# Mixture-of-experts feed-forward on one core: row blocks gathered six ahead into four buffers, three output buffers, and a first run of TensorE products on a tile of ones

## The chip, the cores and the metric

The kernel runs on one core of a Trainium2 chip. A core has a matrix engine (TensorE, PE in the profile, with PEld for its weight loads), VectorE (DVE), ScalarE (ACT), GpSimd (POOL) and SyncE (SP), which here only issues transfers. The metric is the device time of one execution in microseconds; for each kernel the median of its runs is given. The kernel before took 495.78 us (median of 3 runs, 494.04 to 497.90).

## What is computed

The input has 64 batch entries of 64 tokens with 256 features: 4096 tokens. A linear layer with eight low-rank corrections, weighed per batch entry by the condition, gives h. A router picks two of eight experts for each token; an expert is a gated MLP of width 352. A shared MLP of width 704 runs on every token. The output is the input plus both.

```
h      = x @ W_base.T + b_base + 2 * sum_e cond[b, e] * (x @ A_e.T) @ B_e.T
scores = softmax(h @ gate_w.T);  top two, weights normalised, times 2.5
routed = sum over the two experts e: w_e * (silu(h @ w_gate[e]) * (h @ w_up[e])) @ w_down[e]
shared = (silu(h @ sw_gate) * (h @ sw_up)) @ sw_down
out    = x + routed + shared
```

All of it is in float32. Most products are made of three cheaper ones: each operand is split into a high part in a rounded 32-bit format (`_h`) and a low part (`_l`), and `three_pass` (L285) adds high x high, low x high and high x low.

## The kernel before, in words

The program is written out by hand for each engine, and semaphores tie the engines together. An engine runs its instructions in the order written; a wait holds back everything behind it on that engine.

**Start.** SP and ACT issue the loads of the weights (`a_raw`, `base_raw`, `b_raw`) and of the first tokens (`xin`). GpSimd fills the identity tile `ident` (L481, L482). When it is ready, TensorE makes `WARM` = 12 transposes of `ident` into a PSUM bank that nobody reads (L625 to L627). Then it transposes `a_raw` (L632), the first 512 tokens (L640), the gate's weights, the condition and `base_raw` (L654), and makes small float32 products that fold the gate into the linear layer (L658). Those need `gate_t`, which ACT copies after the high parts of the first tokens (`x_high(0)`, L895).

**Projection.** Eight groups of 512 tokens (L677). DVE adds the bias, ACT splits each float32 into two 16-bit halves, and SP writes them to the DRAM tensor `x1_dram`, a row per token.

**Shared MLP, first part.** 5 of the 8 groups go through the shared MLP (L778), each in six chunks. Its sums go by way of `y_sb`, four tiles of 128 x 256 (L145), to `base_dram`; `s_base` counts those stores. Meanwhile DVE works out the routing: `tok_i`, which tokens stand in each block of 128 rows, and `dst_i`, where each row of results goes.

**Routed blocks.** 71 blocks (`NBLK`) of 128 rows, each of one expert. For block i:

- POOL `gather(i)` (L562) fetches the rows by an indirect transfer into `rows[i % 3]`; from block 3 on it waits first for the transpose that read this buffer last (`s_turn`).
- SP `turn_rows(i)` (L349) waits for the gather (`s_row`) and until the words of block i - 2 have been read (`s_rlo`, `s_rhi`), and transposes the rows by DMA into `turned[i % 2]`.
- DVE `r_word_low` (L1354) and ACT `r_word_high` (L1009) put the halves together in `rt_w`; ACT `r_high` and DVE `r_low` split it again for the products.
- PE `e_gate_up(i)` (L806): 12 products, first the gate's, then the up ones. ACT `e_silu` (L1028) and DVE `e_mul` (L1394) follow, the latter into `g`. PE `e_turn_g(i)` (L799) transposes `g`, ACT `e_high` and DVE `e_low` split it, and PE `e_down(i)` (L821) makes the down products. The order on PE is: `e_turn_g(i-1)`, `e_gate_up(i)`, `e_down(i-1)`.
- DVE `e_y(i)` (L1401) adds the two halves of the result into `y_sb[i % 4]`, and POOL `scatter(i)` (L569) writes it to `y_dram` by an indirect transfer. `e_y` of a block from 4 on waits until the scatter of four blocks earlier has landed (`s_sc`); before that it waits for `s_base`.

POOL first issues five gathers; then for each i `gather(i + 5)`, eight times a piece of other work (i = 14 to 21), and `scatter(i)` (L577 to L584).

**End.** The last three groups go through the shared MLP (L870) while SP loads back the routed rows (`load_sums`, L422), once all scatters have landed (L444). DVE adds them in, and the results are stored.

Of the kernel before, what the change touches and what calls it, by code (L numbers as in the profile page):

```python
# [21 lines left out]
def adaln_moe(nc, x, cond, w_base, b_base, lora_a, lora_b, gate_w, w_gate, w_up, w_down,  # L22
              sw_gate, sw_up, sw_down, out):
    NB, SEQ, D = x.shape
    E, RANK, _ = lora_a.shape
# [10 lines left out]
    NBLK = (TOPK * T + E * (P - 1)) // P  # L36
# [3 lines left out]
    TG = GT // P  # L40
# [10 lines left out]
    NPG = 5  # L51
# [2 lines left out]
    UP = NPRE + NBLK  # L54

    TURN = 12
    WARM = 12

    RANK_AT, HOT_AT = 4, 9

# [14 lines left out]
    x1_dram = nc.dram_tensor("x1_halves", (T, 2 * D), U16, kind="Internal").ap()  # L75
# [4 lines left out]
    with ExitStack() as ctx:  # L80
        def sb(name, shape, dt=F32, where=ctx):
            return where.enter_context(nc.sbuf_tensor(name, shape, dt))

        def sem(name):
            return ctx.enter_context(nc.semaphore(name))

        bank = [ctx.enter_context(nc.psum_tensor(f"bank{i}", [P, 512], F32)) for i in range(8)]


        ident = sb("ident", [P, P])  # L90
# [34 lines left out]
        act = sb("act", [P, GT])  # L125
# [13 lines left out]
        rows = [sb(f"rows{i}", [P, 2 * D], U16) for i in range(3)]  # L139
        turned = [sb("turned0", [P, 2 * K, P], U16), turned1]  # L140
# [3 lines left out]
        rt_l = [sb(f"rt_l{i}", [P, D], F32R) for i in range(2)]  # L144
        y_sb = sb("y_sb", [P, TG, D])  # L145

        GU, DN = K * 2 * F, FC * D
# [64 lines left out]
        s_cond, s_gate, s_ath, s_atl, s_wer = (sem(f"s_{n}") for n in ("cond", "gate", "ath", "atl", "wer"))  # L214
        s_wah, s_wal, s_bh, s_bl, s_bg = (sem(f"s_{n}") for n in ("wah", "wal", "bh", "bl", "bg"))
        s_xin = [sem(f"s_xin{i}") for i in range(2)]
        s_xfirst = sem("s_xfirst")
        s_tx, s_txh, s_txl = sem("s_tx"), sem("s_txh"), sem("s_txl")
        s_H, s_hw, s_hwh, s_hwl = sem("s_H"), sem("s_hw"), sem("s_hwh"), sem("s_hwl")
        s_p, s_x1, s_half = sem("s_p"), sem("s_x1"), sem("s_half")  # L220
# [10 lines left out]
        s_res, s_base = sem("s_res"), sem("s_base")  # L231
        s_r, s_exp, s_exp_in = sem("s_r"), sem("s_exp"), sem("s_exp_in")
        s_mark, s_sums, s_rank = sem("s_mark"), sem("s_sums"), sem("s_rank")
        s_ids, s_hot, s_perm, s_routed, s_blk = sem("s_ids"), sem("s_hot"), sem("s_perm"), sem("s_routed"), sem("s_blk")
        s_row = [sem(f"s_row{i}") for i in range(3)]
        s_turn = [sem(f"s_turn{i}") for i in range(2)]
        s_rlo, s_rhi, s_rth, s_rtl, s_gT_e = sem("s_rlo"), sem("s_rhi"), sem("s_rth"), sem("s_rtl"), sem("s_gT_e")
        s_y = sem("s_y")
        s_sc = [sem(f"s_sc{i}") for i in range(4)]
        s_acc = [sem(f"s_acc{j}") for j in range(NG)]  # L240
        s_mix, s_emix, s_out = sem("s_mix"), sem("s_emix"), sem("s_out")

# [11 lines left out]
        EG, EU, TB, YE = bank[0], bank[1], bank[2], bank[6:8]  # L254
# [53 lines left out]
        def _(sp):  # L308
# [39 lines left out]

            def turn_rows(i):  # L349

                sp.wait_ge(s_row[i % 3], 16 * (i // 3 + 1))
                if i >= 2:
                    sp.wait_ge(s_rlo, i - 1)
                    sp.wait_ge(s_rhi, i - 1)
                sp.dma_start_transpose(turned[i % 2][:], rows[i % 3][:]).then_inc(s_turn[i % 2], 16)


            for h, got in enumerate((s_xfirst, s_xin[0])):
# [55 lines left out]
            for i in range(4):  # L414
                turn_rows(i)
            store_base(NPG - 1)
            for i in range(4, NBLK):
                turn_rows(i)
# [22 lines left out]
            sp.wait_ge(s_D, UP)  # L441
            sp.wait_ge(s_base, 16 * NPG)
            load_raw(NPG + 1, raw_p)
            for i in range(4):  # L444
                sp.wait_ge(s_sc[i], 16 * ((NBLK - i + 3) // 4))
            load_sums(NPG)
            load_sums(0)
            load_sums(NPG + 1)
# [15 lines left out]
            for n, (first, end) in ((0, (0, 2)), (2, (3, 4))):  # L464
                sp.wait_ge(s_fin, 2 * last + n + 1)
                r = last * GT
# [5 lines left out]
        def _(pool):  # L472
# [68 lines left out]
            src, d, step = mark, 1, 0  # L541
            while d < NT:
# [3 lines left out]
                src, d, step = dst, 2 * d, step + 1  # L546
# [13 lines left out]


            def gather(i):  # L562
                if i >= 3:
                    pool.wait_ge(s_turn[(i - 3) % 2], 16 * ((i - 3) // 2 + 1))
                pool.indirect_dma_start(rows[i % 3][:], None, x1_dram,  # L565
                                        bass.IndirectOffsetOnAxis(ap=tok_i[:, i:i + 1], axis=0)
                                        ).then_inc(s_row[i % 3], 16)

            def scatter(i):  # L569
                pool.wait_ge(s_y, i + 1)  # L570
                pool.indirect_dma_start(y_dram, bass.IndirectOffsetOnAxis(ap=dst_i[:, i:i + 1], axis=0),  # L571
                                        y_sb[:, i % 4, :], None).then_inc(s_sc[i % 4], 16)

            pool.wait_ge(s_routed, 1)
            for i in range(2):
                pool.wait_ge(s_x1st[i], 16 * (NG // 2))
            for i in range(5):  # L577
                gather(i)
            for i in range(NBLK):
                if i + 5 < NBLK:  # L580
                    gather(i + 5)
                if 14 <= i < 14 + 4 * K:
                    split_low_part(NPG, *divmod(i - 14, 4))
                scatter(i)  # L584
# [4 lines left out]
        def _(pe):  # L589
# [32 lines left out]
                           b_h[:], b_l[:], False, True, skip=True).then_inc(s_p, 1)  # L622


            pe.wait_ge(s_ident, 1)  # L625
            for _ in range(WARM):
                pe.transpose(bank[5][:, 0:P], ident[:], ident[:])  # L627


            pe.wait_ge(s_da, 16)  # L630
# [25 lines left out]
            for k in range(K):  # L656
                for o in range(K):
                    mm = pe.matmul(bank[2 + k][:, D:DX], base_raw[:, o, k * P:(k + 1) * P], gate_t[:, o * E:(o + 1) * E],  # L658
                                   start=(o == 0), stop=(o == K - 1))
# [203 lines left out]
            i = n_turns * TURN + 2  # L863
# [219 lines left out]

        @block.vector
        def _(v):
            v.wait_ge(s_dcond, 16)
            v.tensor_scalar(cond_er[:].rearrange("b (e r) -> b e r", e=E),
                            cond_in[:].rearrange("b (e r) -> b e r", r=1).broadcast_to([NB, E, RANK]),
# [311 lines left out]

            def e_y(i):  # L1401
                v.wait_ge(s_D, UE + i + 1)
                if i < 4:
                    v.wait_ge(s_base, 16 * NPG)
                else:
                    v.wait_ge(s_sc[i % 4], 16 * (i // 4))
                v.tensor_reduce(y_sb[:, i % 4, :], YE[i % 2][:, 0:2 * D].rearrange("p (h d) -> p d h", h=2), AX.X, ALU.add).then_inc(s_y, 1)  # L1407

            r_word_low(1)
            e_mul(0)  # L1410
# [78 lines left out]
```

## Time and profile before

| | before |
|---|---|
| runs | 494.04, 495.78, 497.90 us |
| the profiled execution | 496.81 us, span on the core 495.0 us |
| PE busy | 486.6 us, 98% |
| DVE, ACT, POOL busy | 71%, 53%, 45% |
| DMA | 74.53 MB, mean 151 GB/s |

A row of the timeline gives the start in the span, the duration, engine, line, operation and tiles, with "xN" for merged instructions, and in brackets how long the engine sat idle before and what ended that. Several products can be in flight: the distance between two starts is what one costs in a row, its duration is longer. The start-up takes the first 8 us of the span, the routed blocks lie between about 178 and 424 us.

### The profile page before, as it was taken

What the parts mean: (1) busy time and instruction counts of PE and PEld (TensorE: products, weight loads), DVE (VectorE), ACT (ScalarE), POOL (GpSimd) and SP (SyncE); (2) the same over time, 40 slices, a digit from 0 to 9 for tenths busy, and PEclk for the clock granted to TensorE, in tenths of its full rate; (3) what the DMA queues carried; (4) which work ended last, traced back from release to release, by engine and by line L of the source; (5) the groups of instructions that cost most, each with busy time, mean ns of one, the idle gap of its engine ahead of it and who ended that gap; (6) DMA issues with size and microseconds to landing.
All of it is one profiled execution on the core that took longest, in us unless ns stands there. A gap on an engine that the chain in (4) does not pass through costs nothing.

```text
span 495.0 us, 9758 instructions
## 1 busy us (share of the span) xinstructions
PE 486.6 (98%) x3069; PEld 448.7 (91%) x3070; DVE 349.8 (71%) x785; ACT 261.8 (53%) x526; POOL 220.3 (45%) x231
## 2 busy tenths in 40 slices
PE   8999999999999999899999998999999999999997
PEld 7999988888888899899999998999999999888886
DVE  3557866888886556676777766667766776479896
ACT  3577876666562445475555544555555553444322
POOL 2042338564640444565776555565556552211100
PEclk9999999999999999999999999999999999999999
DMA  7497579372222244444444443444444442599942
GB/s 201 153 299 224 172 204 329 118 219 86 44 85 44 86 106 121 116 118 117 127 118 117 117 126 96 122 115 115 127 117 119 117 118 65 154 376 310 384 159 85
DMA packets 104952, 74.53 MB, mean 151 GB/s; under 512 B 61962, under 2 KB 99860, under 8 KB 104916
## 3 DMA queue, kind: packets, MB, share of 16 engines
q1 hardware_dynamic: 97712, 55.20, 38.4%
q0 software_dynamic: 6816, 18.62, 12.6%
q8 instruction: 17, 0.28, 0.2%
q10 hardware_dynamic: 388, 0.27, 0.2%
q14 instruction: 19, 0.16, 0.1%
HBM read 40.25 MB, written 20.32 MB: 122 GB/s over the span
## 4 chain that ended last, share of the span: by engine, by line
PE 93%; DMA 2%; DVE 2%; issue 1%; ACT 1%; SPq 0%; POOL 0%; DVEq 0%; another core or an unknown queue 0%; POOLq 0%
PE bank L286 22%; PE bank L288 22%; PE bank L287 22%; PE bank L831 10%; PE bank L833 5%; PE bank L803 5%; DMA pick<-y_rows 1%; PE bank L596 1%; PE bank L608 1%; PE bank L604 1%; DMA y_rows<-y_sb,dst_i 1%; PE bank L605 1%; PE bank L741 1%; PE bank L740 1%; DVE acc L1432 1%
## 5 line engine op out<-in xcount | busy, mean ns | idle before, releaser
L571 POOL DMA_INDIRECT y_rows<-y_sb,dst_i x71 | 70.0, 985 | 84.1 <-DVE y_sb L1407 83.8
L286 PE MATMUL bank<-w_all,rt_h 128*128 x284 | 97.5, 343 | 0.0
L288 PE MATMUL bank<-w_all,rt_l 128*128 x284 | 91.6, 323 | 0.0
L287 PE MATMUL bank<-w_all,rt_h 128*128 x284 | 91.5, 322 | 0.0
L565 POOL DMA_INDIRECT rows<-x_halves,tok_i x71 | 68.7, 968 | 25.0 <-issue 21.1
L831 PE MATMUL bank<-w_all,gt_h 128*128 (+1 forms) x213 | 78.1, 397 | 0.0
L1001 ACT CAST gt_h<-bank 128x512 fp32r<-128x512 f32 (+1 forms) x47 | 27.5, 585 | 85.7 <-DVE bank L1310 77.1
L286 PE MATMUL bank<-xs_h,sg_h 128*128 128x512 f32 x176 | 70.4, 400 | 0.0
L287 PE MATMUL bank<-xs_l,sg_h 128*128 128x512 f32 x176 | 68.9, 391 | 0.0
L288 PE MATMUL bank<-xs_h,sg_l 128*128 128x512 f32 x176 | 68.7, 390 | 0.0
L1394 DVE TENSOR_TENSOR g<-bank,act 128x352 f32<-128x352 f32 x71 | 37.2, 525 | 42.3 <-issue 33.8
L1023 ACT CAST gt_h<-bank 128x384 fp32r<-128x384 f32 x71 | 34.0, 479 | 58.1 <-issue 38.4
L1407 DVE TENSOR_REDUCE y_sb<-bank 128x256 f32<-128x512 f32 x71 | 49.0, 690 | 17.4 <-issue 9.7
L833 PE MATMUL bank<-w_all,gt_l 128*128 (+1 forms) x213 | 59.6, 280 | 0.0
L511 POOL TENSOR_TENSOR w_all<-w_own,w_all 128x704 fp32r<-128x704 f32 (+2 forms) x32 | 42.7, 1359 | 32.7 <-ACT w_all L913 32.7
L1014 ACT COPY rt_w<-turned 128x256 uint16<-128x256 uint16 x71 | 34.6, 487 | 41.5 <-PE bank L288 21.3
L287 PEld LDWEIGHTS bank<-w_all,rt_h 128*128 128x128 f32 x284 | 53.6, 189 | 0.0
L286 PEld LDWEIGHTS bank<-w_all,rt_h 128*128 128x128 f32 x284 | 53.5, 189 | 0.1
L288 PEld LDWEIGHTS bank<-w_all,rt_l 128*128 128x128 f32 x284 | 53.4, 188 | 0.0
L1398 DVE TENSOR_TENSOR gt_l<-bank,gt_h 128x384 fp32r<-128x384 f32 x71 | 39.5, 557 | 11.7 <-ACT gt_h L1023 5.7
L517 POOL TENSOR_TENSOR xs_l<-xs_w,xs_h 128x512 fp32r<-128x512 f32 x14 | 18.3, 1308 | 65.6 <-ACT xs_h L935 65.6
L831 PEld LDWEIGHTS bank<-w_all,gt_h 128*128 128x128 f32 (+1 forms) x213 | 40.0, 188 | 6.8 <-issue 0.5
(192 smaller groups left out, 1114.4 us busy)
## 6 DMA issues: line engine op xcount, KB each, us to landing
pick<-y_rows SPq DMA_DIRECT2D x16, 512.0 KB, 7.8
x_halves<-x_half SPq DMA_DIRECT2D x8, 512.0 KB, 3.3
xin<-in_x_dram SPq DMA_DIRECT2D x7, 512.0 KB, 4.8
w_own<-in_L_ffn_w_gate_dram SPq DMA_DIRECT2D x8, 352.0 KB, 4.2
w_own<-in_L_ffn_w_up_dram SPq DMA_DIRECT2D x8, 352.0 KB, 4.7
y_sb<-in_x_dram SPq DMA_DIRECT2D x5, 512.0 KB, 3.4
base_rows<-y_sb SPq DMA_DIRECT2D x5, 512.0 KB, 2.8
acc<-base_rows SPq DMA_DIRECT2D x5, 512.0 KB, 7.5
```

The source lines that it names most:

```text
L286: pe.matmul(o, lh, rh, start=start, stop=False, skip_group_check=skip)
L287: pe.matmul(o, lh, rl, start=False, stop=False, skip_group_check=skip)
L288: return pe.matmul(o, ll, rh, start=False, stop=stop, skip_group_check=skip)
L511: pool.tensor_tensor(lo, own_ap, hi.bitcast(F32), ALU.subtract).then_inc(s_wlo, 1)
L565: pool.indirect_dma_start(rows[i % 3][:], None, x1_dram, bass.IndirectOffsetOnAxis(ap=tok_i[:, i:i + 1], axis=0)).then_inc(s_row[i % 3], 16)
L571: pool.indirect_dma_start(y_dram, bass.IndirectOffsetOnAxis(ap=dst_i[:, i:i + 1], axis=0), y_sb[:, i % 4, :], None).then_inc(s_sc[i % 4], 16)
L831: pe.matmul(YE[par][:, 0:2 * D].rearrange("p (h d) -> p h d", h=2), gt_h[par][0:n, cols], both, start=(c == 0), stop=False, skip_group_che ...
L833: mm = pe.matmul(YE[par][:, 0:D], gt_l[par][0:n, cols], high, start=False, stop=(c == FC - 1), skip_group_check=True)
L1014: sc.copy(words[:, :, :, 1], turned[i % 2][:, K:2 * K, :]).then_inc(s_rhi, 1)
L1394: v.tensor_tensor(g[:, 0:F], EU[:, 0:F], act[:, 0:F], ALU.mult).then_inc(s_g, 1)
L1398: v.tensor_tensor(gt_l[i % 2][:, 0:FC * P], TB[:, 0:FC * P], gt_h[i % 2][:, 0:FC * P].bitcast(F32), ALU.subtract).then_inc(s_gl, 1)
L1407: v.tensor_reduce(y_sb[:, i % 4, :], YE[i % 2][:, 0:2 * D].rearrange("p (h d) -> p d h", h=2), AX.X, ALU.add).then_inc(s_y, 1)
```

## The change

There are two edits.

**The routed blocks' buffers.** The fourth tile of `y_sb` becomes a fourth buffer for gathered rows, so three are left for outputs (`N_Y` = 3). Six gathers are issued first, then `gather(i + 6)` ahead of `scatter(i)`. Block i uses row buffer i for i < 3, and (i + 1) % 4 after that, so block 6 is the first in the shared tile; its gather waits for `s_base` in place of a transpose. From block 7 on `gather(i)` waits for the transpose of block i - 4. `e_y(i)` waits for the scatter of block i - 3.

**The first products.** TensorE no longer waits for `ident` first. DVE fills 128 columns of `act` with 1.0 as its first instruction, and TensorE makes 14 plain products act x act into the same unread bank; only then it waits for `ident`.

```diff
-    WARM = 12
+    WARM = 14
+        N_Y = TG - 1
+        row_bufs = [r[:] for r in rows] + [y_sb[:, N_Y, :].bitcast(U16)]
+
+        def rows_of_block(i):
+            return row_bufs[i if i < 3 else (i + 1) % 4]
...
-                sp.wait_ge(s_row[i % 3], 16 * (i // 3 + 1))
+                sp.wait_ge(s_row[i % 4], 16 * (i // 4 + 1))
...
-                sp.dma_start_transpose(turned[i % 2][:], rows[i % 3][:]).then_inc(s_turn[i % 2], 16)
+                sp.dma_start_transpose(turned[i % 2][:], rows_of_block(i)).then_inc(s_turn[i % 2], 16)
...
             def gather(i):
-                if i >= 3:
-                    pool.wait_ge(s_turn[(i - 3) % 2], 16 * ((i - 3) // 2 + 1))
-                pool.indirect_dma_start(rows[i % 3][:], None, x1_dram,
+                if i == 6:
+                    pool.wait_ge(s_base, 16 * NPG)
+                elif i >= 3:
+
+                    had = i - 3 if i < 6 else i - 4
+                    pool.wait_ge(s_turn[had % 2], 16 * (had // 2 + 1))
+                pool.indirect_dma_start(rows_of_block(i), None, x1_dram,
...
-            for i in range(5):
+            for i in range(6):
                 gather(i)
             for i in range(NBLK):
-                if i + 5 < NBLK:
-                    gather(i + 5)
+                if i + 6 < NBLK:
+                    gather(i + 6)
...
+            pe.wait_ge(s_warm, 1)
+            for _ in range(WARM):
+                pe.matmul(bank[5][:, 0:P], act[:, 0:P], act[:, 0:P], start=True, stop=True)
             pe.wait_ge(s_ident, 1)
-            for _ in range(WARM):
-                pe.transpose(bank[5][:, 0:P], ident[:], ident[:])
...
         def _(v):
+            v.memset(act[:, 0:P], 1.0).then_inc(s_warm, 1)
             v.wait_ge(s_dcond, 16)
...
-                if i < 4:
+                if i < N_Y:
                     v.wait_ge(s_base, 16 * NPG)
                 else:
-                    v.wait_ge(s_sc[i % 4], 16 * (i // 4))
+                    v.wait_ge(s_sc[i % N_Y], 16 * (i // N_Y))
```

PE at the start of the program, of the kernel before (a row is a line, the operation, output and inputs, sizes, and "xN" for repeats):

```order
L588 UNCONDITIONAL_BRANCH
L627 MATMUL bank<-ident 128x128 x12
L632 MATMUL bank<-ident,a_raw 128x128 x2
L640 MATMUL bank<-ident,xin 128x128 x8
L645 MATMUL bank<-ident,g_raw 128x8 x2
```

The same place in the changed kernel, whose lines are numbered about ten higher:

```order
L598 UNCONDITIONAL_BRANCH
L637 MATMUL bank<-act 128x128 x14
L643 MATMUL bank<-ident,a_raw 128x128 x2
L651 MATMUL bank<-ident,xin 128x128 x8
L656 MATMUL bank<-ident,g_raw 128x8 x2
```

Twelve transposes have become fourteen products; nothing else on PE has another order.

POOL from its first gather on, in the kernel before; a DMA into `rows` is a gather and one into `y_rows` a scatter, and the semaphore each waits for stands in brackets:

```order
L565 DMA rows<-x_halves,tok_i 128x512 [waits s_x1st1,s_x1st0,s_routed]
L565 DMA rows<-x_halves,tok_i 128x512 x2
L565 DMA rows<-x_halves,tok_i 128x512 [waits s_turn0]
L565 DMA rows<-x_halves,tok_i 128x512 [waits s_turn1]
L565 DMA rows<-x_halves,tok_i 128x512 [waits s_turn0]
L571 DMA y_rows<-y_sb,dst_i 17408x256 [waits s_y]
L565 DMA rows<-x_halves,tok_i 128x512 [waits s_turn1]
L571 DMA y_rows<-y_sb,dst_i 17408x256 [waits s_y]
L565 DMA rows<-x_halves,tok_i 128x512 [waits s_turn0]
L571 DMA y_rows<-y_sb,dst_i 17408x256 [waits s_y]
```

The same place in the changed kernel, where a gather into the shared tile reads `y_sb<-`:

```order
L575 DMA rows<-x_halves,tok_i 128x512 [waits s_x1st1,s_x1st0,s_routed]
L575 DMA rows<-x_halves,tok_i 128x512 x2
L575 DMA rows<-x_halves,tok_i 128x512 [waits s_turn0]
L575 DMA rows<-x_halves,tok_i 128x512 [waits s_turn1]
L575 DMA rows<-x_halves,tok_i 128x512 [waits s_turn0]
L575 DMA y_sb<-x_halves,tok_i 128x512 [waits s_base]
L581 DMA y_rows<-y_sb,dst_i 17408x256 [waits s_y]
L575 DMA rows<-x_halves,tok_i 128x512 [waits s_turn1]
L581 DMA y_rows<-y_sb,dst_i 17408x256 [waits s_y]
L575 DMA rows<-x_halves,tok_i 128x512 [waits s_turn0]
```

The gather of block 6 has moved ahead of the scatter of block 0, and so every later gather stands one scatter earlier. The transposes that they wait for stand at the same places between the scatters as before.

## Rows read from the trace of the kernel before

**Rows 1.** The page: busy time by engine; chain that ended last, by engine.

```profile
PE 486.6 (98%) x3069; PEld 448.7 (91%) x3070; DVE 349.8 (71%) x785; ACT 261.8 (53%) x526; POOL 220.3 (45%) x231
...
PE 93%; DMA 2%; DVE 2%; issue 1%; ACT 1%; SPq 0%; POOL 0%; DVEq 0%; another core or an unknown queue 0%; POOLq 0%
```

**Rows 2.** Waits of PE: engine, line, releaser: us in total, times, longest.

```profile
PE bank L803 <- DVE g L1394: 3.2, 2, 1.6
PE bank L627 <- POOL ident L482: 1.5, 1, 1.5
```

**Rows 3.** Timeline of the first 8.6 us: start, duration, engine, line, operation, tiles.

```profile
0.80 0.09 POOL L480 MEMSET spare<- 1x4 f32 x1 [0.29 <-POOLq L1479]
...
0.84 0.21 POOL L481 MEMSET ident<- 128x128 f32 x1
1.12 0.29 POOL L482 TENSOR_SCALAR_AFFINE_SELECT ident<-ident 128x128 f32<-128x128 f32 x1
...
1.47 2.82 PE L627 MATMUL bank<-ident 128*128 128x128 f32 x12 [1.47 <-POOL ident L482]
...
4.21 0.29 PEld L632 LDWEIGHTS bank<-ident,a_raw 128*128 128x128 f32 x2 [0.33 <-DMA a_raw<-in_L_cond_As_dram]
...
5.21 0.22 DVE L1087 TENSOR_SCALAR cond_er<-cond_in 64x128 f32<-64x128 f32 x1 [5.21 <-DMA cond_in<-in_cond_dram]
...
6.27 1.07 ACT L895 CAST xt_h<-bank 128x512 fp32r<-128x512 f32 x2 [0.96 <-PE bank L640]
...
7.48 0.97 PEld L658 LDWEIGHTS bank<-gate_t,base_raw 128*128 128x128 f32 x8 [0.30 <-ACT gate_t L944]
```

**Rows 4.** By line: xcount, duration in ns min/median/max, first and last start in us.

```profile
L627 PE MATMUL bank<-ident x12: 421/421/476, 1.5 to 3.9; 128*128 128x128 f32 x12
...
L640 PE MATMUL bank<-ident,xin x8: 273/421/421, 4.7 to 6.1; 128*128 128x128 f32 x8
...
L658 PEld LDWEIGHTS bank<-gate_t,base_raw x8: 186/192/192, 7.5 to 8.3; 128*128 128x128 f32 x8
L658 PE MATMUL bank<-gate_t,base_raw x8: 256/256/277, 7.5 to 8.3; 128*128 128x8 f32 x8
...
L596 PE MATMUL bank<-ident,xin x56: 272/272/307, 12.4 to 54.2; 128*128 128x128 f32 x56
```

**Rows 5.** The page, granted clock in 40 slices; timeline of eight transposes in the projection.

```profile
PEclk9999999999999999999999999999999999999999
...
12.25 0.94 PEld L596 LDWEIGHTS bank<-ident,xin 128*128 128x128 f32 x8
```

**Rows 6.** Critical chain, two of the projection's eight groups of tokens (start, duration, engine, line).

```profile
23.08 0.23 PE bank L604
...
29.80 0.23 PE bank L604
...
36.51 0.23 PE bank L604
```

**Rows 7.** Timeline of PE: the first long wait, and two blocks after it.

```profile
202.98 0.55 PE L803 MATMUL bank<-ident,g 128*128 128x128 f32 x3 [1.60 <-DVE g L1394]
...
206.34 0.49 PE L803 MATMUL bank<-ident,g 128*128 128x128 f32 x3
206.59 0.41 PE L286 MATMUL bank<-w_all,rt_h 128*128 x1
...
209.65 0.49 PE L803 MATMUL bank<-ident,g 128*128 128x128 f32 x3
```

**Rows 8.** Timeline of DVE, ACT and POOL around that wait and behind it.

```profile
199.52 0.41 DVE L1363 TENSOR_TENSOR rt_l<-rt_w,rt_h 128x256 fp32r<-128x256 f32 x1
202.40 0.53 DVE L1394 TENSOR_TENSOR g<-bank,act 128x352 f32<-128x352 f32 x1 [2.46 <-issue]
...
204.56 0.42 DVE L1363 TENSOR_TENSOR rt_l<-rt_w,rt_h 128x256 fp32r<-128x256 f32 x1
...
206.54 0.69 DVE L1407 TENSOR_REDUCE y_sb<-bank 128x256 f32<-128x512 f32 x1
...
200.76 0.46 ACT L1028 ACTIVATE act<-bank 128x352 f32<-128x352 f32 x1 [1.44 <-PE bank L288]
...
207.51 0.99 POOL L571 DMA_INDIRECT y_rows<-y_sb,dst_i  x1 [1.25 <-DVE y_sb L1407]
```

**Rows 9.** Waits for gathered and turned rows: of SP in the span's 173 to 420 us, and of ACT in all.

```profile
SPq L355 <- DMA rows<-x_halves,tok_i: 25.6, 14, 3.0
...
ACT rt_w L1014 <- DMA turned<-rows: 14.0, 18, 1.6
```

**Rows 10.** Critical chain from the last scatter's issue until it has landed.

```profile
423.82 3.76 DMA y_rows<-y_sb,dst_i
```

More of the change, by code:

```diff
@@ L216, in adaln_moe @@
         s_xin = [sem(f"s_xin{i}") for i in range(2)]
-        s_xfirst = sem("s_xfirst")
+        s_xfirst, s_warm = sem("s_xfirst"), sem("s_warm")
         s_tx, s_txh, s_txl = sem("s_tx"), sem("s_txh"), sem("s_txl")
@@ L234, in adaln_moe @@
         s_ids, s_hot, s_perm, s_routed, s_blk = sem("s_ids"), sem("s_hot"), sem("s_perm"), sem("s_routed"), sem("s_blk")
-        s_row = [sem(f"s_row{i}") for i in range(3)]
+        s_row = [sem(f"s_row{i}") for i in range(4)]
         s_turn = [sem(f"s_turn{i}") for i in range(2)]
@@ L238, in adaln_moe @@
         s_y = sem("s_y")
-        s_sc = [sem(f"s_sc{i}") for i in range(4)]
+        s_sc = [sem(f"s_sc{i}") for i in range(N_Y)]
         s_acc = [sem(f"s_acc{j}") for j in range(NG)]
@@ L443, in _ @@
             load_raw(NPG + 1, raw_p)
-            for i in range(4):
-                sp.wait_ge(s_sc[i], 16 * ((NBLK - i + 3) // 4))
+            for i in range(N_Y):
+                sp.wait_ge(s_sc[i], 16 * ((NBLK - i + N_Y - 1) // N_Y))
             load_sums(NPG)
@@ L562, in gather @@
             def gather(i):
-                if i >= 3:
-                    pool.wait_ge(s_turn[(i - 3) % 2], 16 * ((i - 3) // 2 + 1))
-                pool.indirect_dma_start(rows[i % 3][:], None, x1_dram,
+                if i == 6:
[4 more added lines that the diff above has]
+                pool.indirect_dma_start(rows_of_block(i), None, x1_dram,
                                         bass.IndirectOffsetOnAxis(ap=tok_i[:, i:i + 1], axis=0)
-                                        ).then_inc(s_row[i % 3], 16)
+                                        ).then_inc(s_row[i % 4], 16)
             def scatter(i):
@@ L571, in scatter @@
                 pool.indirect_dma_start(y_dram, bass.IndirectOffsetOnAxis(ap=dst_i[:, i:i + 1], axis=0),
-                                        y_sb[:, i % 4, :], None).then_inc(s_sc[i % 4], 16)
+                                        y_sb[:, i % N_Y, :], None).then_inc(s_sc[i % N_Y], 16)
             pool.wait_ge(s_routed, 1)
@@ L1402, in e_y @@
                 v.wait_ge(s_D, UE + i + 1)
-                if i < 4:
+                if i < N_Y:
                     v.wait_ge(s_base, 16 * NPG)
                 else:
-                    v.wait_ge(s_sc[i % 4], 16 * (i // 4))
-                v.tensor_reduce(y_sb[:, i % 4, :], YE[i % 2][:, 0:2 * D].rearrange("p (h d) -> p d h", h=2), AX.X, ALU.add).then_inc(s_y, 1)
+                    v.wait_ge(s_sc[i % N_Y], 16 * (i // N_Y))
+                v.tensor_reduce(y_sb[:, i % N_Y, :], YE[i % 2][:, 0:2 * D].rearrange("p (h d) -> p d h", h=2), AX.X, ALU.add).then_inc(s_y, 1)
             r_word_low(1)
```

## The prediction, made before the changed kernel ran

> **What bounds the kernel.** I read the page's busy times first, then the chain that ended last, then the waits of TensorE, and only then the timelines of the two places that the change touches. TensorE is busy for 486.6 of 495.0 us, and it makes up 93% of the chain [rows 1]. So the reader should ask of each edit one thing: does it let TensorE start its work earlier, do less, or wait less? TensorE's own list of waits is short: 1.5 us for the identity tile at the start, and 3.2 us in two waits for `g` in the routed blocks [rows 2]. The rest of what it is not busy lies behind its last product. Between these, the blocks follow each other at TensorE's own pace: 206.34 to 209.65 us is 3.31 us for a block [rows 7], and 71 blocks of that are 235 us. An edit to the row buffers can win at most the 3.2 us. In the projection the same products come again every 6.72 us (23.08, 29.80, 36.51) [rows 6]: also TensorE's pace, with no slack into which a late start could disappear.
>
> **Row and output buffers.** The transposes that the gathers wait for are the same at each place of POOL's order: at the place ahead of `scatter(i)` both kernels wait for the transpose of block i + 2, and what is fetched there is block i + 5 before and block i + 6 after. So rows stand ready one block, 3.3 us, earlier. Who was late for them? SP waited 14 times, 25.6 us, for gathers, and ACT 18 times, 14.0 us, at most 1.6 us, for turned rows [rows 9]. That is real waiting, but it is covered: `rt_l` of the next block is done at 204.98 (204.56 + 0.42) and TensorE takes it at 206.59 [rows 7, 8], 1.6 us later, and no wait of TensorE in the list ends on `rt_l`. The edit removes covered waits, worth 0. Without that cover each us of lateness beyond it would be a us of TensorE's.
>
> Do the two waits of 1.6 us go? In the first, `rt_l` was finished at 199.93, before the stall; ACT then started the activation late at 200.76, and DVE the product for `g` at 202.40 with nothing that the profile names as its releaser [rows 8]. Neither instruction reads gathered rows or `y_sb`. I take 0; the far bound is -3.2 us.
>
> The price is one output buffer less. The reduce of a block starts at 206.54, its scatter is issued at 207.51 [rows 8], and a scatter takes 3.76 us from issue to landing [rows 10]: 211.27, 4.7 us after the reduce began. The third block after it wants the buffer at 206.54 + 3 x 3.31 = 216.5, so 5.2 us remain; with four buffers it was 8.5. Cost 0. The gather of block 6, now ahead of the first scatter, waits for `s_base`, for which the first `e_y` waits as well; it holds that scatter up by its issue, about 1 us, the same length as the 0.99 of a scatter's [rows 8], well inside the 5.2. The later gathers merely change places with the scatter ahead of them in POOL's queue.
>
> **The first products.** What is gained: DVE is idle until 5.21, so its fill can start when POOL's first own instruction does, at 0.80. POOL's fill of the same size took 0.21, a DVE operation on half the partitions 0.22 [rows 3]; I take 0.20. From the end of the identity (1.12 + 0.29 = 1.41) to the first transpose (1.47) went 0.06 [rows 3]. So the first product starts at 0.80 + 0.20 + 0.06 = 1.06, 0.41 us earlier.
>
> What is paid: the kind of product. The twelve transposes start from 1.5 to 3.9, 11 distances, 0.218 us each [rows 4]. A transpose shows as one record. But L658 is four float32 products in the code, and the trace has eight weight loads and eight products for it [rows 4]: a plain float32 product is two records. Eight of these in a row lie (8.3 - 7.5) / 7 = 0.115 us apart [rows 4], no closer than the eight transposes of L596, of which (0.94 - 0.14) / 7 = 0.115 us [rows 5]. They have only 8 moving columns, so the weight load seems to set the distance; with 128 columns a record can't cost less than that, and as the transposes with 128 columns cost no more, I give each record a transpose's distance. 14 products are then 28 records, where there were 12.
>
> Next the clock. The page prints full granted clock for all slices [rows 5], which hides the start; the durations show it: 421 ns for a transpose at first and 272 later, 0.218 us apart and then 0.115, so TensorE ran at 1.2 GHz and then at 2.4. From the weight load at 4.21 [rows 3] to the last of the ten transposes of L632 and L640 at 6.1 there are nine distances, 1.89 us; n x 0.218 + (9 - n) x 0.115 = 1.89 gives n = 8.3, so the clock rose at about 6.0, 4.5 us after the first transpose, and nothing but transposes had run. After the change I take it at the same distance from the first product, 5.56, or at the same instant, 6.0.
>
> The sum, rise at 5.56: (5.56 - 1.06) / 0.218 = 20.6 records at the slow pace, 7.4 x 0.115 = 0.85 for the others, so L632's successor starts at 6.41 instead of 4.21. Its ten transposes then all run fast; the last starts 9 x 0.115 = 1.03 later, at 7.45, against 6.1: **+1.35 us**. Rise at 6.0: 22.7 records, 5.3 x 0.115 = 0.61, 6.61, 7.65: +1.55. I take +1.4. The load of `a_raw` no longer matters; it was there at 4.21 [rows 3]. What hangs on the transposes, ACT's copy at 6.27 and through `gate_t` L658 at 7.48 [rows 3], moves along, and no later stage gives it back, as TensorE's pace rules there.
>
> Bounds for this term: if the clock were up from the first product, 28 x 0.115 = 3.2, L632 at 4.28, the last transpose at 5.3: -0.8 us. No row shows such a start. The upper bound is the rival below, +4.5.
>
> One rule of the Trainium skill speaks to the price. "TensorE: Matmul & The Clock Gate", in its table of terms, says that transpose mode is "4× faster for FP32". The trace shows two records a product where it shows one for a transpose, at equal distances, which is a factor of 2 for the 8 columns it has; no row has a plain float32 product of 128 columns, so the factor of 4 is open. By the rule the sum would be that of the fourfold rival.
>
> **The sum.** 0 for the buffers + 1.4 for the first products. The profiled execution took 496.81 us, so 498.2 for one like it. It lies 1.03 above the median of 495.78; against the median: 495.78 + 1.4 = **497.2 us**.
>
> **Rivals.**
> (1) *A product costs one transpose.* 14 x 0.218 = 3.05, the row ends at 4.11, L632 starts with `a_raw` at 4.21 as before, and the clock rises 0.4 earlier: 6.2 distances slow, 2.8 fast, the last transpose at 5.88: -0.2 us, 495.6. Against it stand the eight records for four products.
> (2) *A product costs four transposes*, 0.87 slow and 0.46 fast. 4.5 / 0.87 = 5.2 products before the rise, 8.8 x 0.46 = 4.05 after it: 9.6, the last transpose at 10.65: +4.5 us, 500.3. For it: 128 columns instead of 8 may cost each record twice. Against it: in transposes the 128 columns hide behind the weight load.
> (3) *The earlier rows cure the two stalls*, that is, they came from late rows: -3.2 + 1.4 = -1.8, 494.0. Against it: `rt_l` was ready, see above. If the rows edit did that and the start cost nothing, it would be 492.6, still within 1%.
> (4) *Clearly slower: the three output buffers.* If `y_sb` waits for the scatter of three blocks before, TensorE waits too, since `e_down` waits for `s_y` two blocks back. It decides from 9.9 us (3 x 3.31) between reduce and landing; it takes 4.7 now. At 10.2 us a block would cost 3.4 instead of 3.31, 68 blocks x 0.09 = +6 us, 503. Only twice the landing time would do it, and the load on the transfers does not rise.
> (5) *The change does nothing*: both effects under what runs scatter, 495.8.
>
> **Chances and range.** Forecast (+1.4, spread 496.3 to 498.6 with the 1.55 case and the scatter of a median) 0.55; (1) and (5) 0.16; (2) 0.12; (3) 0.10; (4) 0.03; the rest, something unseen of either sign, 0.04. A measurement here can't tell less than about 1%, 5 us, from no change. Below 490.8 lies only unseen gain: 0.03. Above 500.7 lie (4), part of (2) and the unseen: 0.07. Within: 0.90. The range leaves out (4) and the outer parts of (2) and (3): 494.4 to 500.0.
>
> **What would show it.** In the changed kernel's trace: the products on `act` as 28 records, 0.218 us apart and then 0.115, the first at about 1.06; L632's successor at about 6.4 instead of 4.21; `gate_t` products at about 8.8 instead of 7.48, and every later mark 1.4 later. 14 records would make (1) right, distances of 0.4 or more (2). In the blocks: SP's and ACT's waits for rows shrink towards nothing, the block stays at 3.31 us, and POOL's and DVE's waits for `s_sc` don't appear. I am wrong if TensorE's waits for `g` vanish together with the late rows, if the clock is already up in the first products, or if a wait of TensorE for `y_sb` turns up.

## The result, and the profile after

The changed kernel takes 501.01 us (median of 6 runs, 499.76 to 501.81), the kernel before beside it 495.28 (6 runs, 493.35 to 498.57): 5.7 us more, ratio 1.010 with a 95% interval of 1.0064 to 1.0137. The forecast was 497.2 and no measurable change, its range ended at 500.0. The slower time lies outside. The ratios, here and in the table below, are taken from the runs no more than 1.5% above the fastest of the same kernel; in the second series this leaves out 15 of the 35 runs of the kernel before (the other 20 have a median of 498.08) and 3 of the 12 of start_again (the other 9: 501.81), elsewhere at most one run of a kernel.

A difference in microseconds is one of medians. The recorded ratio is not the quotient of the two medians, and can differ from it: after_third's medians are 1.8 us apart, its ratio of 1.0049 would be 2.4.

The profiled execution took 501.19 us with a span of 499.2, against 496.81 and 495.0. The busy times of the page, to be held against [rows 1], and TensorE's waits, against [rows 2]:

```profile
PE 489.0 (98%) x3085; PEld 451.0 (90%) x3086; DVE 349.9 (70%) x786; ACT 262.5 (53%) x526; POOL 221.2 (44%) x231
```

```profile
PE bank L814 <- DVE g L1406: 3.2, 2, 1.7
PE bank L814 <- issue: 1.5, 2, 0.9
PE bank L637 <- DVE act L1097: 1.1, 1, 1.1
PE bank L292 <- DVE gt_l L1331: 0.6, 1, 0.6
```

There are 16 more instructions on PE (28 records for 12), and two more kinds of wait stand in the list: 1.5 us ahead of the transposes of `g` (L814, which was L803) without a releaser that the profile names, and 0.6 us near the end. The start, to be held against [rows 3]:

```profile
0.90 0.17 DVE L1097 MEMSET act<- 128x128 f32 x1 [0.90 <-PEq L1491]
1.12 5.58 PEld L637 LDWEIGHTS bank<-act 128*128 128x128 f32 x28 [0.79 <-DVE act L1097]
...
6.62 0.25 PEld L643 LDWEIGHTS bank<-ident,a_raw 128*128 128x128 f32 x2
...
9.12 0.97 PEld L669 LDWEIGHTS bank<-gate_t,base_raw 128*128 128x128 f32 x8 [0.31 <-ACT gate_t L955]
```

The products need the time up to 6.6; `a_raw`, there at 4.21 before, waits for TensorE now. The weight loads of L669 start at 9.12 against 7.48: 1.64 us late. The loss of 4.2 us of span falls in three places: 1.6 at the start; some 2.0 in the routed blocks (the first transposes of `g` come 1.6 us later than before, the last ones 3.6); and 0.6 after them. The three places in the blocks where TensorE stood longest:

```profile
205.41 0.55 PE L814 MATMUL bank<-ident,g 128*128 128x128 f32 x3 [1.66 <-DVE g L1406]
...
375.25 0.55 PE L814 MATMUL bank<-ident,g 128*128 128x128 f32 x3 [0.94 <-issue]
...
383.67 0.55 PE L814 MATMUL bank<-ident,g 128*128 128x128 f32 x3 [1.59 <-DVE g L1406]
```

The first is the counterpart of the wait at 202.98 [rows 7]: in both kernels it stands ahead of the transposes of block 5 (the blocks counted from 0). The other wait of the kernel before, at 304.11, is gone, and two others have come: the second row stands behind block 55, the third two blocks further on. Rows are not late there. SP's waits in the routed blocks (span 173 to 420) show that they are early:

```profile
SPq L360 <- DVE rt_w L1371: 110.5, 52, 4.1
SPq L360 <- ACT rt_w L1025: 5.1, 3, 2.8
```

The 25.6 us for gathers of [rows 9] are gone, and SP waits for the words of block i - 2 instead: the gathered rows lie ready and the two `turned` buffers are what is scarce. ACT's 14.0 us for turned rows, 18 waits, are down to 2.0 us in two waits.

### The profile page after: what moved, and what is told of

Same layout as the page of the kernel before. It is cut to its first block, busy times and chain, and to the rows that moved or that the text cites. A ratio compares the mean times of both kernels' runs of the same rounds, so it can differ in the third digit from the quotient of the medians.

```text
span 499.2 us, 9791 instructions
## 1 busy us (share of the span) xinstructions
PE 489.0 (98%) x3085; PEld 451.0 (90%) x3086; DVE 349.9 (70%) x786; ACT 262.5 (53%) x526; POOL 221.2 (44%) x231
## 4 chain that ended last, share of the span: by engine, by line
PE 92%; DMA 2%; DVE 2%; issue 2%; ACT 0%; SPq 0%; another core or an unknown queue 0%; DVEq 0%
PE bank L292 22%; PE bank L293 22%; PE bank L294 22%; PE bank L842 10%; PE bank L844 5%; PE bank L814 5%; DMA pick<-y_rows 1%; PE bank L606 1%; PE bank L637 1%; DMA y_rows<-y_sb,dst_i 1%; PE bank L618 1%; PE bank L614 1%; PE bank L615 1%; PE bank L752 1%; PE bank L751 1%
## 5 line engine op out<-in xcount | busy, mean ns | idle before, releaser
L575 POOL DMA_INDIRECT rows<-x_halves,tok_i x54 | 52.5, 973 | 19.5 <-DMA turned<-rows 10.2
```

Of the source, the lines that this page charges most:

```text
L575: pool.indirect_dma_start(rows_of_block(i), None, x1_dram, bass.IndirectOffsetOnAxis(ap=tok_i[:, i:i + 1], axis=0)).then_inc(s_row[i % 4], 16)
```

## Experiments

A series is a set of kernels run in turn with the kernel before, on one chip. The series differ: in some the kernel before lies within 492 to 494 us nearly always (quiet), in others it scatters by 5 to 15 us. I speak of quiet chips and chips that stall, but that it is the chip, and not the hour, is not shown: only one chip was used twice (third and last series), and was quiet both times. In the profiles the difference lies in stalls of 1 to 2 us in the routed blocks. It turned out to decide what the change costs, so each row names its series. The start_warm28 and no_warm rows rest on four runs each. "First", "second", "third" and "fourth" in the expectations are the series that hold the changed kernel itself.

| series, kernel before (median, lowest to highest, runs) | kernel | median us | ratio to before (95%) |
|---|---|---|---|
| first, 495.28 (493.35 to 498.57, 6) | changed kernel | 501.01 | 1.0100 (1.0064 to 1.0137) |
| parts, quiet, 492.79 (491.77 to 496.83, 29) | start_only | 494.26 | 1.0042 (1.0025 to 1.0059) |
| | start_warm7 | 492.83 | 1.0011 (0.9995 to 1.0026) |
| | rows_only | 493.02 | 1.0003 (0.9979 to 1.0027) |
| | outputs3_only | 492.73 | 1.0001 (0.9992 to 1.0011) |
| second, 500.86 (494.0 to 508.92, 35) | after_again | 503.04 | 1.0047 (1.0017 to 1.0078) |
| | both_warm7 | 501.59 | 1.0058 (1.0014 to 1.0101) |
| | start_again | 503.13 | 1.0057 (1.0007 to 1.0106) |
| | rows_again | 501.63 | 1.0041 (1.0007 to 1.0074) |
| third, quiet, 492.84 (491.8 to 496.21, 12) | after_third | 494.65 | 1.0049 (1.0035 to 1.0063) |
| | ident_products | 494.55 | 1.0025 (1.0003 to 1.0048) |
| | start_warm28 | 499.49 | 1.0135 (1.0115 to 1.0156) |
| | no_warm | 496.53 | 1.0081 (1.0066 to 1.0097) |
| fourth, 495.64 (493.47 to 501.22, 23) | before_copy | 495.65 | 0.9997 (0.9964 to 1.0029) |
| | after_fourth | 500.55 | 1.0094 (1.0063 to 1.0126) |
| | both_warm7_again | 499.18 | 1.0063 (1.0039 to 1.0087) |
| last, quiet, 492.74 (491.71 to 496.47, 27) | rows_third | 492.73 | 1.0008 (0.9997 to 1.0019) |
| | outputs3_again | 492.83 | 1.0004 (0.9995 to 1.0013) |
| | rows_scatter_first | 492.69 | 0.9988 (0.9969 to 1.0007) |

### The parts alone

The start edit alone, in the kernel before:

```diff
-    WARM = 12
+    WARM = 14
+            pe.wait_ge(s_warm, 1)
+            for _ in range(WARM):
+                pe.matmul(bank[5][:, 0:P], act[:, 0:P], act[:, 0:P], start=True, stop=True)
             pe.wait_ge(s_ident, 1)
-            for _ in range(WARM):
-                pe.transpose(bank[5][:, 0:P], ident[:], ident[:])
...
+            v.memset(act[:, 0:P], 1.0).then_inc(s_warm, 1)
```

> The start edit alone: 14 products of ones, three row buffers and four output buffers as before. The changed kernel's trace shows 28 records of products and every later mark of the projection 1.6 us later, but the whole is 5.7 us slower in the median. Theory A (the start costs its 1.65 us and no more; the rest of the loss is made by the row buffers): +1.6 us, 497. Theory B (the start edit costs everything, because a later stage falls out of step): +5.7, 501. Theory C (two small costs and the scatter of the runs): +1.6 here and about +2 with the rows edit alone.

+1.5 us: theory A's number, and theory B is dead for a quiet chip. The same with 7 products:

```diff
-    WARM = 14
+    WARM = 7
```

> The start edit alone with 7 products in place of 14, so 14 records. If a record costs the distance of a transpose (0.2 us at first), the row of them ends at about 4.1 us and the load of a_raw, there at 4.2, comes last again: 0 to -0.3 us against before by theories A and C (the shift of the start is all that the edit does). Theory B has no reason for a loss either if it hangs on the shift; if it hangs on plain products or on the tile of ones as such, it stays 3 to 5 us slower.

No difference. So the loss hangs on the number of products. The products' own rows, of start_warm7 and then of start_only (x, duration min/median/max in ns, first and last start in us):

```profile
L627 PEld LDWEIGHTS bank<-act x14: 288/333/333, 1.1 to 3.8; 128*128 128x128 f32 x14
```

```profile
L627 PEld LDWEIGHTS bank<-act x28: 192/270/333, 1.1 to 5.6; 128*128 128x128 f32 x28
```

Fourteen records for 7 products, 28 for 14. The last of the 28 starts here at 5.6, in the changed kernel of the first series at 6.5: more of them fell into the fast clock (12 of the distances are 0.11 us here, 3 there).

The buffer edit alone is the changed kernel with the old start:

```diff
+            pe.wait_ge(s_ident, 1)
+            for _ in range(WARM):
+                pe.transpose(bank[5][:, 0:P], ident[:], ident[:])
-            pe.wait_ge(s_warm, 1)
-            for _ in range(WARM):
-                pe.matmul(bank[5][:, 0:P], act[:, 0:P], act[:, 0:P], start=True, stop=True)
-            pe.wait_ge(s_ident, 1)
...
-            v.memset(act[:, 0:P], 1.0).then_inc(s_warm, 1)
```

> The buffer edit alone: six gathers ahead into four buffers, three for outputs, with the twelve transposes of the identity at the start as before. Theory A: +4 us, 499, with TensorE's waits in the routed blocks grown by as much in most profiles (the changed kernel's profile has 6.3 us over 70 regular blocks, that of the kernel before 4.3). Theory B: 0. Theory C: about +2.

Nothing, on this chip. And the half of it that takes an output buffer away, with gathers as before:

```diff
-                if i < 4:
+                if i < N_Y:
...
-                    v.wait_ge(s_sc[i % 4], 16 * (i // 4))
-                v.tensor_reduce(y_sb[:, i % 4, :],
+                    v.wait_ge(s_sc[i % N_Y], 16 * (i // N_Y))
+                v.tensor_reduce(y_sb[:, i % N_Y, :],
```

> Three output buffers alone: gathers as before, five ahead into three buffers, and the fourth tile of y_sb left idle in the routed blocks. If the loss of the buffer edit comes from waits for a free output, it is here too, as large as in the buffer edit alone. If it comes from the gathers that run one block further ahead (other transfers at other times, GpSimd's scatters behind a gather's wait), this one takes 0 against before. My reading of the slack (5 us) says 0.

Nothing either. TensorE's list of waits in rows_only holds no wait in the blocks at all. Theory A's +4 us and theory C's +2 for the buffer edit both missed here. The parts add up to +1.5 to +2, not to 5.7.

### The whole again, on a chip that stalls

> The changed kernel itself, unaltered, again beside the kernel before. Alone, the start edit has cost 1.5 us in the median and a ratio of 1.0042, and the buffer edit nothing. Theory A (the two edits add up, and the rest of the 5.7 us measured first were stalls of 1.7 us that fell on its executions more often): +1.5 to +2, ratio 1.003 to 1.005, and its profile has no or few late semaphores of TensorE. Theory D (the two edits together make something that neither makes alone, a stage that falls out of step): +5 or more, ratio 1.010 or more, with waits of TensorE in the routed blocks in most executions.

> Both edits, with 7 products in place of 14 (14 records, which end at about 4.1 us, before a_raw is there). Theory A: the start costs nothing any more, so the kernel is as fast as before, ratio 0.998 to 1.002. Theory D, an interaction of the buffers with products of ones at the start: slower by 3 us or more still.

> The start edit alone once more, in the same series as the changed kernel, to compare the two directly. Theory A: the same time as the changed kernel within 0.5 us, ratio to before about 1.004. Theory D: 3 us or more below the changed kernel.

> The buffer edit alone once more, in the same series. Theory A: ratio 0.998 to 1.002. If the buffer edit makes the kernel more liable to stalls where the chip has them, the median or the highest time is above that of the kernel before by 2 us or more; the number of executions over 494.5 us tells it, where the kernel before had 3 of 29 in the last series.

The kernel before now took 501 us in the median and scattered from 494 to 509. The changed kernel was 2.2 us slower, as theory A has it, but both edits with 7 products came out at 1.0058 and the buffer edit alone at 1.0041, where A says 1.000. Against the 498.08 named with the result, the medians of the changed kernel, of both edits with 7 products and of the buffer edit alone are 5.0, 3.5 and 3.6 us up, which is what the fourth series will show; but start_again's 501.81 is 3.7 up too, where its edit explains 1.6. With intervals of plus or minus 0.4% this series can't decide, and I did not settle on A.

### What the row of products costs

> The changed kernel unaltered, a third series. The first gave ratio 1.0100 (1.0064 to 1.0137), the second 1.0047 (1.0017 to 1.0078). Theory A (1.6 us of start, the rest stalls that don't belong to the edits): ratio 1.003 to 1.005, +1.5 to +2.5 us. Theory D (a real loss of 4 us or more): 1.008 or more.

1.0049 on a quiet chip, +1.8 us: there the changed kernel costs what its start costs.

```diff
-                pe.transpose(bank[5][:, 0:P], ident[:], ident[:])
+                pe.matmul(bank[5][:, 0:P], ident[:], ident[:], start=True, stop=True)
```

> The kernel before with one word changed: the twelve first instructions are products of ident with ident in place of transposes. Nothing starts earlier, only the kind changes: 24 records in place of 12. If the kind is what costs: the records run to about 6.3 instead of 3.9 us with the clock up at 5.9 as in the profile of before, and the whole is 1.0 to 1.6 us slower. If the loss of the start edit came from the tile of ones or from VectorE's fill: no change.

+1.7 us in the median by this one word. Neither the tile of ones nor VectorE is to blame, the kind of product is. Its row, 24 records for 12 products and up to 5.7, where the 12 transposes of [rows 4] end at 3.9:

```profile
L627 PEld LDWEIGHTS bank<-ident x24: 192/333/338, 1.5 to 5.7; 128*128 128x128 f32 x24
```

Doubling the row (`WARM = 28` in start_only):

> The start edit alone with 28 products in place of 14, 56 records. By the theory that only the length of this row counts, 28 more records at the fast distance of 0.11 us add 3.1 us to the +1.5 of 14 products: +4.6 against before, ratio about 1.009. If a later wait took up a late start, it would be less.

+6.6 us, more than the 4.6 expected. The start is as worked out: `a_raw`'s transposes at 9.00, where the kernel before has them at 4.2. The rest stands in the profile as waits in the routed blocks, where start_only had none:

```profile
PE bank L832 <- DVE gt_l L1400: 2.7, 3, 1.4
```

VectorE makes `gt_l`, and the trace names what had held VectorE up. Ahead of the first of the three waits it was the first `e_y`, which waits for the last store out of `y_sb` (`s_base`), 2.60 us where start_only has 1.20. Ahead of the last it was a wait for turned rows:

```profile
194.21 0.69 DVE L1409 TENSOR_REDUCE y_sb<-bank 128x256 f32<-128x512 f32 x1 [2.60 <-DMA base_rows<-y_sb]
...
413.80 0.32 DVE L1361 COPY rt_w<-turned 128x256 uint16<-128x256 uint16 x1 [2.18 <-DMA turned<-rows]
```

TensorE waited 1.44 and 1.04 us behind these two. So a late start can cost more than itself, and rows that come late can hold up TensorE; why these transfers were late in this profile, no run here shows. And with no first transposes at all (`WARM = 0` in the kernel before):

> The kernel before without any of the twelve first transposes. TensorE starts with a_raw, there at 4.2 us. If the clock rises at a distance from the first work as it did (2.9 to 5.8 us in the profiles so far), it is up at 7 to 10 us instead of 4 to 7, three us later, in which TensorE works at half speed in parts: +0.5 to +1.5 us. If the twelve transposes do nothing for the clock: 0.

+3.7 us, more than twice the most I expected. TensorE starts with `a_raw`, works with gaps, and is still at 1.2 GHz long after. A run of products and one of transposes at the end of the slow stretch:

```profile
15.11 0.42 PE L288 MATMUL bank<-wa_h,xt_l 128*128 128x264 f32 x1
15.33 0.61 PE L668 MATMUL bank<-ident,b_raw 128*128 128x128 f32 x2
...
16.59 0.64 PE L596 MATMUL bank<-ident,xin 128*128 128x128 f32 x4
```

The products of 264 columns are 0.22 us apart up to 15 us, where the changed kernel and the kernel before have 0.12 at 11 and 10 us; the transposes at 16.6 are fast. The clock rose at about 15.8 us, against 4 to 7 in the profiles with a first row. So that row of transposes is worth 3.7 us. The two rows that cost nothing, 12 transposes and 7 products, both end at about the time when `a_raw` is there; a shorter row was not tried.

### Is the rest the chip's, or the change's?

> The kernel before, letter for letter, measured as if it were a changed one. Where executions scatter little, ratio 1.000 within 0.002. Where they scatter by 10 us, as in the second series (494 to 509 us), theory A says that even this copy can come out 2 to 4 us away from its original, and that this is the size of what is left unexplained of the first series.

> The changed kernel unaltered, a fourth series, beside the copy. Theory A: 1.003 to 1.006 where executions scatter little; with stalls, that plus or minus what the copy shows. Theory D: 1.008 or more against the original and the copy.

> Both edits with 7 products. Theory A: the loss of the changed kernel is its 28 records at the start, so with 14 it is at the time of before: ratio 0.998 to 1.002 where executions scatter little, and 1.5 us below the changed kernel in any series. In the second series it was 1.4 us below in the median.

This decided against theory A. On a chip where the kernel before scatters from 493 to 501 us, its copy came out at 0.9997, the changed kernel at 1.0094 and both edits with 7 products at 1.0063, +3.5 us. The start with 7 products cost nothing on a quiet chip (1.0011), so I put the 3.5 us down to the buffers; the buffer edit alone was not run in this series, and its 1.0041 (1.0007 to 1.0074) in the second is the only such time on a chip that stalls. Over 12 runs each, the lowest is 497.0 where the copy's is 493.3, and the highest 500.3 where the copy's is 501.3: it is the undisturbed runs that are missing. The profiles say where. Both have the pair of long waits of the first series, of after_fourth and then of both_warm7_again:

```profile
373.93 0.55 PE L814 MATMUL bank<-ident,g 128*128 128x128 f32 x3 [0.96 <-issue]
...
382.37 0.33 PE L814 MATMUL bank<-ident,g 128*128 128x128 f32 x1 [1.61 <-DVE g L1406]
```

```profile
374.40 0.55 PE L814 MATMUL bank<-ident,g 128*128 128x128 f32 x3 [0.94 <-issue]
...
382.77 0.55 PE L814 MATMUL bank<-ident,g 128*128 128x128 f32 x3 [1.54 <-DVE g L1406]
```

They stand at the same two blocks in all six profiles with the buffer edit from the three series that scatter (the changed kernel three times, both_warm7 twice, rows_again). From the transposes of block 55 to those of 56, and from 57 to 58, it takes 4.4 and 5.1 us in place of 3.3, so the pair costs 2.9 us. The three profiles without the edit from these series (before, start_again, before_copy; the next expectation says four, which is a miscount) have stalls too, two in each, but never this pair: behind blocks 4 and 34 in before, 4 and 54 in start_again, 8 and 26 in before_copy. (A stall behind one of the blocks 2 to 4 is in all six as well. Up to the transposes of block 5 they lose 2.3 to 4.2 us, the three without the edit 0.7 to 2.3.) Those of before_copy:

```profile
216.21 0.55 PE L803 MATMUL bank<-ident,g 128*128 128x128 f32 x3 [1.22 <-DVE g L1394]
...
276.49 0.55 PE L803 MATMUL bank<-ident,g 128*128 128x128 f32 x3 [0.61 <-issue]
```

A long stall can cost once more through the clock. In both_warm7_again TensorE stood for 2.08 us, and then the granted clock was 0.50 (1.2 GHz) from 196.2 to 199.6 us, in the middle of the blocks:

```profile
196.40 0.90 PE L814 MATMUL bank<-ident,g 128*128 128x128 f32 x3 [2.08 <-DVE g L1406]
...
196.20:199.60 3.40, 3.20 (x12) 3.19 (x13) 1.83 (x5) 1.34 (x4) 1.87 (x2) 0.50 0.27 77
```

The next transposes come 4.8 us later, not 3.3. In rows_again the granted clock was 0.50 from 9.2 to 12.6 us, and the first transposes of `g` come at 186.07, 2.2 us later than in rows_only. The mean granted clock of each run hints how often that happens: it is 0.998 or less in 10 of the 18 runs with the buffer edit in this series, in 6 of the 35 without, and in 1 of the 60 of the last, quiet series.

### Which half of the buffer edit

> The buffer edit alone, a third series. So far it cost nothing where executions scatter little (1.0003), while both edits with 7 products cost 1.0063 in the fourth series, where the kernel before scattered from 493 to 501 us and its copy was at 0.9997. In all six profiles with the buffer edit from series that scatter, TensorE lost 1.1 us after block 55 and 1.7 us after block 57; none of four without the edit has that pair. Theory E (the buffer edit makes stalls of its own, on chips that have stalls): where the kernel before scatters by 5 us or more, +2.5 to +3.5 us, ratio 1.005 to 1.007, with the pair in the profile; on a quiet chip 0 and no pair. Theory A (no effect): 0 everywhere.

> Three output buffers alone, again. If theory E holds by the fewer outputs, it shows the same loss and the same pair at blocks 55 and 57 as the buffer edit beside it. If it holds by the gathers that run one block further ahead, it is at 1.000 with no pair. I expect the latter, since no wait for an output buffer stands in any profile.

The order on GpSimd turned round, in the buffer edit alone:

```diff
-                if i + 6 < NBLK:
-                    gather(i + 6)
                 if 14 <= i < 14 + 4 * K:
                     split_low_part(NPG, *divmod(i - 14, 4))
                 scatter(i)
+                if i + 6 < NBLK:
+                    gather(i + 6)
```

> The buffer edit alone, with GpSimd's order turned round: in each step first the scatter of block i, then the gather of block i + 6 (the same distance in transfers as before the edit, with one row buffer more). If the loss of theory E hangs on when GpSimd's gathers and scatters go out, the pair of stalls at blocks 55 and 57 goes or moves and the ratio falls by 0.003 or more against the buffer edit beside it; if it hangs on the four buffers as such, it stays.

The chip was a quiet one, and all three are at 1.000. The buffer edit alone has no pair there; at the blocks in question its transposes come every 3.3 us:

```profile
372.23 0.49 PE L813 MATMUL bank<-ident,g 128*128 128x128 f32 x3
...
375.53 0.49 PE L813 MATMUL bank<-ident,g 128*128 128x128 f32 x3
...
382.14 0.49 PE L813 MATMUL bank<-ident,g 128*128 128x128 f32 x3
```

That agrees with theory E for a quiet chip and tells nothing about the halves. Which of them makes the pair, and whether GpSimd's order does, stays open.

## Why the prediction was wrong

**The bound.** Right. TensorE's order and pace set the time outside the stalls: a start 1.6 us late reached the end, and earlier rows gained nothing.

**The first products.** Mechanism right, size nearly. The first product was foreseen at 1.06 and came at 1.12 (VectorE's fill, foreseen at 0.80, started at 0.90), the records are 28 as foreseen, 0.21 us apart and then 0.11. Foreseen: +1.4; measured: +1.64 in the profile, +1.5 alone and +1.8 as a whole on quiet chips. That a record of 128 columns costs no more than a transpose was a choice from a row of 8 columns; it held. Rivals (1) and (2) fall with it. The Trainium skill, "TensorE: Matmul & The Clock Gate", in its table of terms, has transpose mode "4× faster for FP32". This case does not show it: a product is two records 0.21 us apart, a transpose one at 0.21 after the last, a factor of 2 at 128 columns; 14 records of 7 products end where 12 transposes did. What I treated as a constant is none: the instant of the clock's rise. In the profiles with a first row it lies anywhere between 4 and 7 us, with transposes as with products, so the earlier first product bought nothing that these runs can tell.

**The buffers: "The edit removes covered waits, worth 0", and "Cost 0".** This step failed, and only on some chips. What its working names held: SP's waits for gathers vanished, ACT's for turned rows fell from 14.0 to 2.0 us, no wait for an output buffer appeared (outputs3_only: 1.0001), and on quiet chips the whole edit costs nothing (1.0003, 1.0008). What it left out is that the two stalls of [rows 7, 8] were a sign of something that the edit could also make worse. I had noted that neither stalled instruction reads rows or `y_sb`, concluded that the edit would not touch them, and gave only the case in which they go. In the series that scatter, the edit comes with a pair of such stalls at fixed blocks, 2.9 us a time, and +3.5 us in the median of the fourth series with 7 products. With the 1.6 of the start that is 5.1, against 4.9 in the fourth series and 5.7 in the first. Why the edit brings the pair stays open. Nor does the cover always hold: in start_warm28, with three row buffers, a wait of 2.18 us for turned rows cost TensorE 1.04. In the second the difference was 2.2, within a scatter of 15 us of the kernel before.

**The base.** Another failing of the same kind: I took one profile's stalls as part of a constant time. The kernel before itself lies at 492.8 us on quiet chips; the 496.81 of its profiled execution held some 3 us of stalls. Of a time with such a share one should say first what of it is work and what is stall, and what each edit does to either.

**The rivals.** The three output buffers (4) never came near: no wait in any profile. That both edits do nothing (5) is true of the buffer edit in the quiet series alone. Rival (2) has 500.3, close to the 501.01, but by luck: no record is 0.4 us from the last. The cure of the two stalls (3) did not come about. The stated range, 494.4 to 500.0, is also narrower than the 490.8 to 500.7 that the chance of 0.90 was worked out for; the measured time lies above both.

## What to carry to other kernels

A first row of work that brings up TensorE's clock should end when the first operand is there, and not later: here 12 transposes (or 7 float32 products) do, 14 products cost 1.5 us, and none at all costs 3.7. Count it in records of the trace; a plain float32 product is two. A kernel that leaves no slack should be measured on more than one chip, beside a copy of itself, before a half per cent is believed: the same changed kernel was 1.0049 in a quiet series and 1.0094 in one that scattered. Where the waits that a prefetch removes never reach the engine that sets the pace, it has nothing to gain, and here it came with a loss.

## What the runs showed of the hardware

The stalls in the blocks look the same in all profiles that have them: TensorE's products are recorded on time, but what waits for them starts late. Around the first of the pair in the changed kernel, the last up product of block 56 on PE, then DVE, then ACT:

```profile
372.93 0.32 PE L294 MATMUL bank<-w_all,rt_l 128*128 x1
...
373.08 0.39 PE L842 MATMUL bank<-w_all,gt_h 128*128 x1
```

```profile
372.35 0.42 DVE L1375 TENSOR_TENSOR rt_l<-rt_w,rt_h 128x256 fp32r<-128x256 f32 x1
374.67 0.53 DVE L1406 TENSOR_TENSOR g<-bank,act 128x352 f32<-128x352 f32 x1 [1.90 <-issue]
```

```profile
372.33 0.47 ACT L1039 ACTIVATE act<-bank 128x352 f32<-128x352 f32 x1 [0.18 <-PE bank L294]
374.67 0.48 ACT L1025 COPY rt_w<-turned 128x256 uint16<-128x256 uint16 x1 [1.87 <-PE bank L294]
```

The product ends at 373.25 by its record. `act` was ready at 372.80. The next instructions of DVE and ACT both wait for the semaphore `s_U` that this product raises, and both start at 374.67, 1.4 us later, in the same 10 ns. The trace's own record of this semaphore's update stands at 374.59, 1.34 us behind the product's recorded end; the median of TensorE's updates is 0.014 behind. In the kernel before the same gap is 2.1 us (DVE at 202.40 [rows 8]), behind this product:

```profile
200.00 0.32 PE L288 MATMUL bank<-w_all,rt_l 128*128 x1
```

So what is late is the signal, or the product's true end behind its recorded one; nothing here tells these apart, nor why chips differ, nor why the buffer edit pins two of the stalls behind blocks 55 and 57. In the eleven profiles of the quiet series no update of TensorE is late by 0.4 us or more, not in start_warm28 either, so its waits are of another kind.

One thing more sets the two sorts of series apart: the nine traces of those that scatter hold 4903 to 5020 records of semaphore updates, the eleven of the quiet ones 7435 to 7473, though the instructions are all there in both. Whether the taking of the profile has a part in the stalls is a rival that no run here excludes. Packets of program code come during blocks 56 and 57 in all twenty profiles, the quiet ones too, so they alone don't make the pair.
